# Four graph layers over one 4096 x 4096 adjacency: later-neighbour counts taken from partition bases and running sums

## The reference

```python
support = input @ weight
mask = (adj != 0)
rank = cumsum(mask, axis=1); deg = rank[:, -1:]
k = minimum(deg, 100.0); pos = rank - (deg - k)
w = mask * where(pos > 0, 0.5 ** (k - pos), 0.0)
out = w @ support + bias
```

## Time and profile before

| | us |
|---|---|
| median of 3 runs (lowest, highest) | 1661.46 (1649.61, 1664.8) |
| the profiled execution's own time | 1657.53 |
| its span | 1655.5 |
| PE busy | 1501.7 (91%) |
| DVE busy | 1173.1 (71%) |
| ACT busy | 946.2 (57%) |
| POOL busy | 306.4 (19%) |

### The profile page before, as it was taken

The page is one execution under the profiler, slowest core; times in us unless marked ns, Lnnn a source line. Parts: engine busy times, 40 slices in busy tenths (PEclk is TensorE's granted clock), DMA queues, the critical chain, the costliest instruction groups (busy, mean ns, idle before and its releaser), DMA issues.

```text
span 1655.5 us, 20803 instructions
## 1 busy us (share of the span) xinstructions
PE 1501.7 (91%) x7945; PEld 636.2 (38%) x7990; DVE 1173.1 (71%) x1579; ACT 946.2 (57%) x918; POOL 306.4 (19%) x154
## 2 busy tenths in 40 slices
PE   5999999989999699999999999989788889889870
PEld 1433333333333444444444454434333333333330
DVE  4777755557888565765856846567888888888867
ACT  1243488853343423323334336767889898998954
POOL 1000000000000000000000002685445444444430
PEclk9999999999999699999999999999999999999995
DMA  9999779969999335443442431245344554544500
GB/s 340 412 413 412 301 308 409 409 259 365 412 413 369 117 116 190 153 155 143 161 153 105 173 130 49 79 135 190 123 137 161 165 178 134 173 133 151 165 13 26
DMA packets 118106, 348.95 MB, mean 211 GB/s; under 512 B 6324, under 2 KB 31224, under 8 KB 117752
## 3 DMA queue, kind: packets, MB, share of 16 engines
q1 hardware_dynamic: 106784, 329.27, 53.1%
q10 hardware_dynamic: 11224, 18.36, 3.0%
HBM read 329.78 MB, written 17.83 MB: 210 GB/s over the span
## 4 chain that ended last, share of the span: by engine, by line
PE 60%; issue 15%; POOL 11%; DVE 7%; DMA 3%; ACT 2%; SPq 0%; POOLq 0%; DVEq 0%; ACTq 0%
PE ps L777 17%; PE ps L904 13%; POOL ring L674 11%; PE ps L910 10%; PE ps L716 3%; DMA ring<-in_adjT 3%; PE ps L715 3%; PE ps L933 2%; PE ps L849 2%; PE ps L741 1%; PE ps L939 1%; PE ps L731 1%; PE ps L797 1%; DVE work L1698 1%; DVE work L1685 1%
## 5 line engine op out<-in xcount | busy, mean ns | idle before, releaser
L904 PE MATMUL ps<-ring,X 128*64 128x512 f32 x512 | 264.1, 598 | 13.3 <-DVE ring L1946 13.3
L1187 ACT ACTIVATE work<-ps,code_bias 128x1024 uint8<-128x1024 f32 x128 | 135.8, 1111 | 243.4 <-PE ps L716 234.9
L905 PE MATMUL ps<-work,X 128*64 128x512 f32 x512 | 264.1, 597 | 0.0
L635 POOL TENSOR_SCALAR work<-ring 128x1024 int16<-128x1024 uint8 x24 | 69.5, 2907 | 1022.1 <-DMA ring<-codes 976.3
L1318 ACT ACTIVATE work<-ring 128x2048 f32<-128x2048 f32 x64 | 122.2, 1911 | 216.6 <-PE ps L912 195.7
L674 POOL TENSOR_TENSOR ring<-ring,work 128x1024 f32<-128x1024 f32 x80 | 190.0, 2375 | 249.0 <-DVE work L2202 248.8
L910 PE MATMUL ps<-work 128*64 128x512 bf16 x768 | 208.3, 380 | 0.0
L912 PE MATMUL ps<-work 128*64 128x512 bf16 x768 | 208.2, 380 | 0.0
L1006 PE MATMUL ps<-work 128*128 128x512 f32 x320 | 163.4, 634 | 0.0
L777 PE MATMUL ps<-ring,work 128*64 128x512 f32 x704 | 160.8, 598 | 1.6 <-DMA ring<-in_adjT 1.6
L1943 DVE TENSOR_SCALAR work<-ring 128x2048 bf16<-128x2048 f32 x64 | 78.5, 1226 | 106.8 <-PE ps L912 106.5
(11 more groups left out here) (332 smaller groups left out, 2646.6 us busy)
## 6 DMA issues: line engine op xcount, KB each, us to landing
ring<-in_adjT SPq DMA_DIRECT2D x90, 2048.0 KB, 11.2
work<-in_adjT SPq DMA_DIRECT2D x26, 2048.0 KB, 18.6
ring<-in_adjT SPq DMA_DIRECT2D x48, 1024.0 KB, 8.0
codes<-work ACTq DMA_DIRECT2D x64, 256.0 KB, 6.1
ring<-codes SPq DMA_DIRECT2D x32, 512.0 KB, 3.6
ring<-in_adjT SPq DMA_DIRECT2D x32, 512.0 KB, 3.6
X<-in_x ACTq DMA_DIRECT2D x1, 1024.0 KB, 6.7
work<-in_xT SPq DMA_DIRECT2D x2, 512.0 KB, 23.3
```

The costliest lines, as they stand in the source:

```text
L904: nc.tensor.matmul(ps[0:F, h, :], rows, ring[:, r, k, cols], start=start, stop=stop)
L905: nc.tensor.matmul(ps[F:P, h, :], rows, negs[:, pair, i, cols], start=start, stop=stop)
L1187: nc.scalar.activation(codes[:, u, k:k + 2, :].rearrange("p k c -> p (k c)"), ps[:, bank:bank + 2, :].rearrange("p k c -> p (k c)"), ACT.Relu,
```

## The change

The nodes are numbered anew by the host: block `b`, partition `p` holds node `N - 1 - (32 p + b)`. Each partition then holds 32 neighbouring nodes, in descending order. The number of later neighbours of a node is what the partitions before it hold (`base`, one matmul of the mask with a triangular matrix), plus a running sum over the blocks of its own partition.

- Pass 0 writes masks of whole tiles and PE accumulates `base` (`add_base`); no codes. ACT copies `base` out once a quarter.
- Pass 2 runs the sums over the first half of the columns: a chain of one DVE operation a block; ACT makes the byte of each sum, neighbour or not. PE has no work for it. The tiles come in rising order now, so the first one needs the last quarter of `T2`.
- The second half of the columns is done in the second layer: two links of the chain, one ACT operation and one store of 128 KB for each pair. Tiles are read in rising order, and the diagonal is cut pair by pair where it comes.
- As codes no longer know who is a neighbour, the third layer multiplies with differences of `support` of neighbouring nodes: the weight of a neighbour is twice the difference of two successive powers. Block 0 needs a row of the last block, so it has a late step of its own (`first_support`, `split_first`) and tile 0 of quarters 0 and 1 moves behind tiles 1 to 3. The byte is now multiplied by 128 and 128 added.

```diff
+                elif self.p == 1 and q == NQ - 1:
+                    self.g = (6, 7, 0, 1, 2, 3, 4, 5)[self.s]
                 else:
-                    self.g = self.s if self.p == 1 else NS - 1 - self.s
+                    self.g = self.s if self.p else NS - 1 - self.s
...
-                                        code_in[:, i % RING, :, 3, :], 128.0, None, ALU.mult).then_inc(decay_pool, 1)
+                                        code_in[:, i % RING, :, 3, :], CODE_STEP, CODE_STEP, ALU.mult,
+                                        ALU.add).then_inc(decay_pool, 1)
                 if i == 14:
                     pool.wait_ge(normed[1], NQ)
-                    pool.wait_ge(support_ready, NQ)
+                    pool.wait_ge(support_ready, NQ + 1)
...
-            def rank(a):
...
-                    nc.tensor.matmul(ps[:, bank, :], later_or_self[:], mask[:, u, k, :], start=True, stop=False)
-                    mm = nc.tensor.matmul(ps[:, bank, :], minus_ones[:], later[:, u, j, :], start=False, stop=True)
...
+            def add_base(a):
+                u, bank = a.t % 2, 2 + 4 * (a.q % 2)
+                pe.wait_ge(mask_made, a.t + 1)
+                if a.s == 0 and a.q >= 2:
+                    pe.wait_ge(base_read, 2 * (a.q - 1))
+                for h in range(2):
+                    for k in range(GB):
+                        mm = nc.tensor.matmul(ps[:, bank + h, :], earlier[:], mask[u][:, k, h * HALF:(h + 1) * HALF],
+                                              start=a.s == 0 and k == 0, stop=a.s == NS - 1 and k == GB - 1)
+                mm.then_inc(based, 1)
...
+                        nc.tensor.matmul(ps[:, 2, 2 * c:2 * c + 2], count_in[:, c * P:(c + 1) * P], pick[:],
+                                         start=True, stop=False)
+                        mm = nc.tensor.matmul(ps[:, 2, 2 * c:2 * c + 2], totals[row, c * P:(c + 1) * P], halves[row, :],
+                                              start=False, stop=True)
...
+                if a.t == 2 * SLOTS:
+                    turn(a.turn - 1)
...
-            pe.wait_ge(linked_summed, 2 * NQ)
-            for b in range(NB):
-                q, h, c = b // CB, b % CB // GB, b % GB
-                mm = nc.tensor.matmul(ps[:, 2, NB + b:NB + b + 1], linked_in[:, q, h, c * P:(c + 1) * P], ones[:, 0:1],
...
+                    if n or j:
+                        before = h2T[:, (j - 1) * P:j * P] if j else edge_T[:, 0:P]
+                        mm = nc.tensor.matmul(ps[:, 4, j * P:j * P + F], before, w2_before[:, 0:F], start=False, stop=True,
+                                              skip_group_check=True)
                 mm.then_inc(support_ready, 1)
+            def first_support():
+                pe.wait_ge(support_read, NQ)
+                pe.wait_ge(edge_turned, NQ + 4)
+                nc.tensor.matmul(ps[:, 4, 0:F], edge_T[:, 0:P], w2_before[:, F:2 * F], start=True, stop=True)
+                nc.tensor.matmul(ps[:, 4, F:2 * F], edge_T[0:F, P:2 * P], w2_sb[0:F, 0:F], start=True,
+                                 stop=True).then_inc(support_ready, 1)
...
+                u, n = a.n % 2, a.n
+                act.wait_ge(later_made, later_after(a.q, GB * a.s + GB - 1))
...
+                nc.scalar.activation(codes[:, u, k:GB, :].rearrange("p k c -> p (k c)"),
+                                     later[:, u * GB + k:(u + 1) * GB, :].rearrange("p k c -> p (k c)"), ACT.Relu,
+                                     bias=code_bias[:], scale=-1.0).then_inc(codes_made, 1)
...
+            def make_codes1(q, m):
+                n, u = q * PAIRS + m, m % 2
+                act.wait_ge(later_made, later_after(NQ + q, 2 * m + 1))
+                act.wait_ge(codes_stored[u], (NS * NQ // 2 + n // 2) * 16)
...
+                nc.scalar.activation(codes1[:, u, first:], two[:, first:], ACT.Relu, bias=code_bias[:],
+                                     scale=-1.0).then_inc(codes_made, 1)
+                act.wait_ge(codes_made, codes1_after(n))
+                act.dma_start(codes_dram[q * NS + m // 2, 1][:, u * QC:(u + 1) * QC], codes1[:, u]).then_inc(
+                    codes_stored[u], 16)
...
+                V.tensor_scalar(mask[a.n % 2], a.room, 0.0, None, ALU.not_equal).then_inc(mask_made, 1)
+                add_rows(a, a.rows[0], slice(0, QC))
...
+            def make_later(a):
+                n = a.n
...
+                for k in range(GB):
+                    j = GB * a.s + k
+                    if j < NB - 1:
+                        if k == GB - 1 and n:
+                            dve.wait_ge(codes_made, codes_after(n - 1))
+                        dve.wait_ge(later_made, later_after(a.q, j))
+                        V.scalar_tensor_tensor(later[:, (j + 1) % (2 * GB), :], a.room[:, k, 0:HALF], 0.0,
+                                               later[:, j % (2 * GB), :], ALU.not_equal, ALU.add).then_inc(later_made, 1)
+                    if k < 2:
+                        add_rows(a, a.rows[0], slice(k * HALF, (k + 1) * HALF))
...
+            def open_chain(q):
+                if q:
+                    dve.wait_ge(codes_made, codes1_after(q * PAIRS - 2))
+                V.tensor_scalar(later1[:, 0, :], base[:, 1, q, :], not_first[:], None, ALU.mult).then_inc(later_made, 1)
+            def extend_chain(q, j, edges):
+                if j == NB - 1:
+                    return
+                last = q * PAIRS + (j - 3) // 2
+                if last >= 0:
+                    dve.wait_ge(codes_made, codes1_after(last))
+                dve.wait_ge(later_made, later_after(NQ + q, j))
+                V.scalar_tensor_tensor(later1[:, (j + 1) % GB, :], edges, 0.0, later1[:, j % GB, :], ALU.not_equal,
+                                       ALU.add).then_inc(later_made, 1)
...
+                    if s // 2 == q:
+                        mine = own_blocks(ring[:, r], s % 2, pair)
...
+                        extend_chain(q, 2 * m, edges[:, 0, HALF:QC])
+                        dve.wait_ge(diag_steps, 2 * m + 1)
+                        V.tensor_reduce(diag[:, 2 * m:2 * m + 2], own, AX_X, ALU.add).then_inc(diag_steps, 1)
...
+                        extend_chain(q, 2 * m + 1, edges[:, 1, HALF:QC])
+                        dve.wait_ge(later_made, later_after(NQ + q, min(2 * m + 2, NB - 1)))
...
+                        dve.wait_ge(pair_used, q * PAIRS + m + 1)
+                        dve.wait_ge(diag_cut, m + 1)
...
+                        extend_chain(q, 2 * m, edges[:, 0, HALF:QC])
+                        dve.wait_ge(pair_used, q * PAIRS + m + 1)
+                        V.tensor_scalar(more[:, pair], edges, 0.0, None, ALU.is_gt)
+                        extend_chain(q, 2 * m + 1, edges[:, 1, HALF:QC])
+                        V.tensor_scalar(less[:, pair], edges, 0.0, None, ALU.is_lt)
...
+def node_order():
+    return N - 1 - np.arange(N).reshape(P, NB).T.reshape(-1)
```

377 lines of the change are left out of this document (221 added, 156 removed).

## The result

| | before | the change |
|---|---|---|
| median (20 runs each; lowest, highest) | 1657.96 (1648.69, 1668.17) | 1664.53 (1659.91, 1673.9) |
| ratio of runs, 95% interval | | 1.0044 [1.0025, 1.0064] |
| span of the profiled execution | 1655.5 | 1662.4 |

What follows compares the result with a forecast made beforehand. PE was taken as the bound, with DMA close behind in the second and third passes. 1657.5 - 20.2 + 8.4 + 4.3 = 1650.0, plus 3.9 from execution to median, gave 1654 us; 8-in-10 range 1636 to 1680.

Steps and rivals of the forecast that it cites:

- Third pass: First layer's last pass: 59 us of PE work removed, loads and stores then set the pace; last turn 19.2 us sooner.
- Second pass: First layer: eight more small matmuls a turn cost between 0 and 3 x 1.84 us; taken as 0, hidden by loads.
- Hand-over: Second to third pass: the turn now precedes the first tile's product, so loads restart at 369.3 us, not 362.1.
- First pass, 0: First layer: eight base matmuls replace eight rank matmuls, DVE's 3.7 us a tile stays under 5.42; no change.
- Second layer: Links hidden in ordinary pairs, but diagonal pairs at 6.15 us exceed PE's 6.02; +8.4 us, ends +2.5 and +23.
- Third layer: Extra work before the first product and POOL's later clearings; +4.3 us together, between 1 and 7.
- The 3 us for tile 15: Third layer: later POOL clearings make tile 15's part 4.2 us late for PE, of which about 3 remain.
- POOL's second operation: Third layer's byte conversion: taken as 0, double as other end; rival with POOL as bound about 1690 us, chance 0.12.
- the cast and the multiplication at one price: Third layer, POOL: 1480 and 1485 ns for the same size, so an added operation was taken to cost 0.
- The rule cited beside it: Trainium skill on POOL loops: up to two operations an element bound by ports; cited against the POOL rival, chance 0.12.
- Stores don't take the loads' time: Rival, third pass: code stores travel beside loads without slowing them, another 15 us gained, about 1638 us; chance 0.17.
- The clock in the third pass: Rival: PE's gaps drop the clock to 1.2 GHz, products take 7.3 us, total about 1715 us; chance 0.05.

Runs made afterwards that it cites:

- short_stores: Changed kernel, but the third pass stores only a quarter of each tile's codes (64 KB for 256), the rest filled by copies in the second layer; 1654.62 us, one run.
- grouped: Changed kernel, but each second-pass turn issues its eight count-table matmuls first, then the eight with the totals' row, instead of by turns; 1662.72 us, one run.
- thin_links: Changed kernel with the second layer's chain links 16 columns wide instead of 512, except the first four; 1663.59 us, one run.
- one_op: Changed kernel with the added 128 moved from the conversions of all engines into the byte, so POOL converts with one operation; 1666.97 us, ratio 1.0041 to the kernel before.
- mixed: Changed kernel with the byte one higher, no 128 added, POOL converting with one operation up to its two clearings and two behind them; 1661.77 us.

## Why the prediction was wrong

- **Third pass: right.** Loads and stores of 5.7 us a tile pace it (short_stores: 14 us for 15 us of bytes), 59 us of rank matmuls bring what the DMA leaves, DVE's link costs 0.69. From the first load to the last turn it took 161.1 us, with 160.2 forecast.
- **Second pass: this step failed.** It said that three turns cost "between 0 and 3 x 1.84" and "I take 0, since the loads' 133 us and their late start hide them". The pass got 13.9 us longer (from 136.7 to 150.6 between the same two tiles of the chain). Two mistakes. The cover was not there: 133 us of loads beside 150 of pass is 17 us of lead for PE, not level, and the chain before left PE for a load once, for 1.9 us in all. And the price was too low by more than half: a turn costs 3.0 us of matmuls (1.8 for their number, 1.2 for the alternation, by grouped), and by the lower clock behind them 1.0 to 2.3 us more in the next product and 0.3 to 0.9 in the count and the small matmuls beside it. Of these even my upper end had only the 1.84. Over three turns PE's own time grew by 15.7 us, and loads had covered 1.9 of it.
- **Hand-over: right in kind, low in size.** The first product starts 7.1 us later in relation to the pass's last tile, where 6.0 was forecast; the small matmuls again.
- **First pass, 0: not refuted.** The second pass begins 2.9 us later in the profile of the changed kernel, where a product at 70.35 took 6.19 us at a granted clock of 0.58. But of the eight profiles with this first pass, five begin the second pass sooner than the kernel before (208.5 to 209.8, for 210.8), so the 2.9 us lie within what executions of equal code differ by.
- **Second layer:** +3.3 for +8.4. The links are shown to be 2.3 of it (thin_links). The size was too high: a diagonal pair came out just under PE's period, not just over, and what the first quarter was to lose, 2.0 us, was 0.
- **Third layer:** +6.9 for +4.3, of other parts. The 3 us for tile 15 behind the late clearings did not come: the clearings ended 12 us later, but PE does not wait for POOL there, with the fast conversions or with the slow ones (one_op). PE waits once for POOL in the layer, 1.50 us at 1151.29, 49 us behind the clearings, at the tile where the kernel before waits 1.10 (1144.14). In its place stand 5.0 us ahead of the second half, and the 1.8 us that PE waits for ACT's copy in the late step, where the prediction had only the work ahead of the first product. Of the 5.0 I read from the timeline, and did not test, that PE waits 2.31 us for the normalisation (0.32 before) and that the further `support` matmuls make 1.2 us of PE into 2.0; mixed takes back 0.4.
- **Rivals:** POOL's second operation was to cost nothing or double. It made the conversion 2.5 times as fast, outside both ends; the argument from the cast and the multiplication at one price was sound for what it compared and said nothing of this form. The rule cited beside it, by which one operation and two should cost the same, is not borne out either. "Stores don't take the loads' time" is refuted by short_stores. The clock in the third pass does fall, to 0.91 in two windows, and costs nothing while the loads are slower still; where it cost was the second pass, which no rival had. (Its price was also mis-added: 234 for 165 us on 1654 is 1723, not 1715.)

## What to carry to other kernels

Two resources at 100% in a window are not level: the chain of waits says which one holds, and how often it leaves it, and only its waits for the other are cover for new work. An instruction added to a queue that is on the chain at every tile costs its time, its alternation with differently shaped neighbours, and what it does to the clock of those behind it. A gain in a stage that is paced by a stream starts where the stream starts: look first at what delays the first load.

## What the runs showed of the hardware

- POOL's `tensor_scalar` from uint8 to int16, 128 x 1024, takes 2.76 to 3.3 us with one operation (mean 2907 ns) and mostly 1.04 us (mean 1142 to 1178 ns) with two, even when the second adds zero.
- A DVE operation of 128x512 f32 with two SBUF inputs takes 0.69 us. If it starts within 0.68 us (slow form) or 0.94 us (fast form) behind the start of such a conversion, it takes 1.30 to 1.57; if it starts later into one, it keeps 0.68 to 0.81. Both forms hold it up.
- Small f32 matmuls, 2 columns wide, cost 0.23 us each in a row of one shape (1.85 us for eight of 128 rows, 1.94 for eight of one row) and 0.305 us by turns. Behind 1.84 us of them the next product kept its 3.65 us; behind 3.65 to 4.87 us of them it took 4.6 to 6.0, at a granted clock down to 0.60 (from 343 to 350 us in the changed kernel).
